# A product over 12500 entities in fp32: pieces of 4 tiles with a ramp and a taper against rounds of 2, 2, 2 and 1 tiles

## The reference

```python
entities = jnp.einsum('be,le->bl', entity_idxs, W)    # x 1024 x 12500, W 128 x 12500, fp32
s = jnp.sum(entity_idxs, axis=1)
s_safe = jnp.where(s != 0, s, 1.0)
scale = jnp.where(s != 0, 1.0 / s_safe, 1.0)
return entities * scale[:, None]
```

## Time and profile before

| | |
|---|---|
| median of 3 runs | 151.33 us |
| the profiled execution | 151.15 us, span 149.4 |
| TensorE matmul, weight load | 135.2 us (91%), 76.4 (51%), 785 each |
| VectorE, ScalarE, GpSimd | 94.5 us (63%), 84.1 (56%), 0.7 |
| DMA | 58.19 MB in 5719 packets, mean 390 GB/s |
| loads in `xw` | 20 of 2304 KB, median 16.3 us from issue to landing |

### The profile page before, as it was taken

How to read it: one execution, slowest core, us unless ns; L and a number is a source line. 1 busy time by engine, 2 the same in 40 slices (tenths; PEclk the granted TensorE clock), 3 DMA queues, 4 the chain that set the end, 5 groups by cost and what they waited for, 6 DMA issues and landing times.

```text
span 149.4 us, 2230 instructions
## 1 busy us (share of the span) xinstructions
PE 135.2 (91%) x785; PEld 76.4 (51%) x785; DVE 94.5 (63%) x110; ACT 84.1 (56%) x129; POOL 0.7 (0%) x13
## 2 busy tenths in 40 slices
PE   0597998799999999999999999999999999999960
PEld 0244654455555555555555655655555555665530
DVE  0471953746756845955954954864864778965593
ACT  3571852735735834844843854763763677955173
POOL 1000000000000000000000000000000000000000
PEclk9999999999999999999999999999999999999998
DMA  5999999999999999999999999999999999999022
GB/s 147 404 427 459 405 454 399 449 420 425 444 410 449 410 444 420 434 434 410 454 415 434 420 439 429 410 459 410 434 425 439 408 425 416 414 406 342 16 70 75
DMA packets 5719, 58.19 MB, mean 390 GB/s; under 512 B 638, under 2 KB 1534, under 8 KB 2514
## 3 DMA queue, kind: packets, MB, share of 16 engines
q1 hardware_dynamic: 5714, 58.13, 92.6%
HBM read 57.60 MB, written 0.52 MB: 389 GB/s over the span
## 4 chain that ended last, share of the span: by engine, by line
DMA 56%; PE 35%; DVE 4%; SPq 1%; issue 1%
DMA xw<-main 56%; PE acc L417 35%; DVE y_sum L366 2%; DVE low_max L320 1%; SPq L167 1%; DVE row_sum L363 0%; SPq L163 0%; SPq L165 0%; DVE row_sum L357 0%; DVE row_sum L360 0%; DVE any_low L396 0%; PE acc L470 0%; DVE inexact L398 0%
## 5 line engine op out<-in xcount | busy, mean ns | idle before, releaser
L417 PE MATMUL acc<-parts_main,xw 128*128 128x385 bf16 x640 | 108.2, 327 | 3.8 <-DMA xw<-main 3.0
L417 PEld LDWEIGHTS acc<-parts_main,xw 128*128 128x128 bf16 x640 | 61.3, 98 | 50.7 <-issue 8.4
L320 DVE TENSOR_REDUCE low_max<-xw 128x2048 uint16 x20 | 45.5, 2278 | 0.0
L243 ACT ACTIVATE parts_main<-xw 128x512 bf16<-128x512 bf16 x20 | 12.7, 635 | 47.0 <-DMA xw<-main 37.7
L309 DVE TENSOR_TENSOR w_rest<-xw 128x512 f32<-128x512 f32 x20 | 13.8, 692 | 40.0 <-DMA xw<-main 40.0
L250 ACT ACTIVATE act_out<-xw 128x2048 bf16<-128x2048 uint16 x20 | 37.9, 1893 | 0.0
L316 DVE TENSOR_TENSOR parts_main<-w_rest 128x512 bf16<-128x512 f32 x21 | 14.6, 695 | 0.7
L246 ACT ACTIVATE parts_main<-w_rest 128x512 bf16<-128x512 bf16 x21 | 13.3, 635 | 2.0
L417 PE MATMUL acc<-parts_short,xw_short 84*128 84x385 bf16 x8 | 2.7, 522 | 5.5 <-ACT parts_short L246 5.5
L320 DVE TENSOR_REDUCE low_max<-xw_taper 128x1 f32<-128x1024 uint16 (+1 forms) x6 | 6.1, 1038 | 1.4 <-DMA xw_taper<-ends 1.3
L250 ACT ACTIVATE act_out<-xw_taper 128x1024 bf16<-128x1024 uint16 (+1 forms) x6 | 5.4, 906 | 1.7 <-DMA xw_taper<-ends 1.6
(11 more groups left out here) (50 smaller groups left out, 38.2 us busy)
## 6 DMA issues: line engine op xcount, KB each, us to landing
xw<-main SPq DMA_DIRECT2D x20, 2304.0 KB, 16.3
xw_taper<-ends SPq DMA_DIRECT2D x2, 1024.0 KB, 24.9
x_final<-ends SPq DMA_DIRECT2D x3, 512.0 KB, 27.8
xw_taper<-ends SPq DMA_DIRECT2D x1, 1408.0 KB, 21.8
xw_ramp<-ends SPq DMA_DIRECT2D x1, 1280.0 KB, 7.5
xw_taper<-ends SPq DMA_DIRECT2D x1, 1280.0 KB, 18.8
xw_taper<-ends SPq DMA_DIRECT2D x2, 512.0 KB, 27.1
xw_ramp<-ends SPq DMA_DIRECT2D x1, 704.0 KB, 4.9
```

The costliest lines, as they stand in the source:

```text
L243: nc.scalar.activation(parts[0:rows, 0:n, 0:L], top(words, n), ACT.Copy)
L320: nc.vector.tensor_reduce(low_max[0:rows, bass.ds(col, 1)], low(words, n), AX.XY, ALU.max).then_inc(dve_checked, 1)
L417: return nc.tensor.matmul(acc[:, b, 0:N], x, parts, start=first, stop=last)
```

## The change

The pieces become a uniform loop. After the short tile and the first two W tiles (`w_first`), 13 rounds of four pieces with 2, 2, 2 and 1 x tiles follow (52 pieces, 91 tiles), each with the W tiles of the next piece (2, 2, 1 and 2). There are still four slots, now with buffers of the pieces' own sizes. Then come the last four W tiles alone (`w_alone`) and the last 6 x tiles, cut by banks as before. Ramp and taper are gone. TensorE's program text has 8 products for the short tile, 56 for a round, 48 for the final tiles, and ahead of them a loop of 12 products of a zeroed tile (`idle`) into `acc`, which the first real products overwrite. In the final part VectorE checks a quarter of the words and ScalarE three quarters, `finish` adds the parts of both banks of a pair in one instruction, and the last bank is scaled by VectorE.

```diff
+IDLE_PRODUCTS = 12
+ROUNDS = 13
+SLOT_X = (2, 2, 2, 1)
+SLOTS = len(SLOT_X)
+SLOT_W = SLOT_X[1:] + SLOT_X[:1]
+PIECES = ROUNDS * SLOTS
+LAST = 6
+FINAL = ((0, 2, 0, 6), (2, 4, 0, 6), (4, 6, 0, 6), (6, 7, 0, 6), (7, 8, 0, 4), (7, 8, 4, 6))
+PAIRS = ((0, 2), (2, 4), (4, 6), (6, 7), (7, 8))
+ALONE = LAST - SLOT_X[0]
...
+            nc.gpsimd.memset(idle[:, :], 0.0).then_inc(idle_set, 1)
...
+            sp.dma_start(xw_short[0:short, :], edge(0)).then_inc(short_in, 16)
+            sp.dma_start(w_first[:, :], edge(1)).then_inc(first_in, 16)
             for s in range(SLOTS):
-                load_main(s, s)
-            with sp.Fori(1, MAIN // SLOTS) as i:
+                sp.dma_start(xw[s][:, :], piece(0, s)).then_inc(loop_in[s], 16)
+            with sp.Fori(1, ROUNDS) as i:
                 for s in range(SLOTS):
                     m = SLOTS * i + s
+                    sp.wait_ge(products_done, used(m - SLOTS))
+                    sp.wait_ge(dve_checked, used(m - SLOTS))
+                    sp.wait_ge(act_checked, used(m - SLOTS))
+                    sp.dma_start(xw[s][:, :], piece(i, s)).then_inc(loop_in[s], 16)
+            sp.dma_start(w_alone[:, :], edge(2)).then_inc(alone_in, 16)
...
 # ScalarE
+            with act.Fori(0, ROUNDS) as i:
                 for s in range(SLOTS):
                     m = SLOTS * i + s
+                    act.wait_ge(loop_in[s], 16 * (i + 1))
+                    act.wait_ge(products_done, used(m + 1 - SLOTS))
+                    split(xw[s][:, XS[s]:], parts[(s + 1) % SLOTS], SLOT_W[s], (s + 1) % 2, unit_split(m + 1))
+                    act.wait_ge(act_checked, used(m - 2))
+                    low_sum(xw[s][:, XS[s] // 2:XS[s]], m + 1, (s + 1) % 2).then_inc(act_checked, 1)
+            act.wait_ge(alone_in, 16)
+            split(w_alone, parts_alone, ALONE, 1, ALONE_SPLIT)
...
+            check(0)
+            check(1)
+            scale(0)
+            check(2)
+            scale(1)
+            check(3)
+            check(4)
+            scale(2)
+            check(5)
+            scale(3)
 # VectorE
+            dve.wait_ge(alone_in, 16)
+            dve.wait_ge(top_parts_done, unit_split(PIECES - 1))
+            rest(w_alone[:, :], ALONE, 1)
+            lo(parts_alone, ALONE, 1, ALONE_SPLIT)
...
             def finish(pair):
                 b0, b1 = PAIRS[pair]
+                dve.wait_ge(bank_full, pair + 1)
+                row_sum_is_zero(b0, b1, ONES).then_inc(sum_step, 1)
+                add_parts(b0, b1).then_inc(y_summed, 1)
...
+            check(0)
+            check(1)
+            finish(0)
+            check(2)
+            finish(1)
+            check(3)
+            check(4)
+            finish(2)
+            check(5)
+            finish(3)
+            finish(4)
+            dve.wait_ge(inverse_done, len(PAIRS))
+            dve.wait_ge(y_summed, len(PAIRS))
+            nc.vector.tensor_scalar(y[:, BANKS - 1, :], y_sum[:, BANKS - 1, :], row_sum[:, BANKS - 1, 2:3], None,
+                                    ALU.mult).then_inc(y_last_ready, 1)
 # TensorE
+            pe.wait_ge(idle_set, 1)
+            with pe.Fori(0, IDLE_PRODUCTS):
+                nc.tensor.matmul(acc[:, 0, 0:N], idle[:, 0:P], idle[:, :], start=True, stop=True)
             pe.wait_ge(ones_set, 1)
             pe.wait_ge(short_in, 16)
+            wait_split(1)
+            multiply(xw_short[0:short, 0:B], 1, parts_short, rows=short, first=True).then_inc(products_done, 3)
+            with pe.Fori(0, ROUNDS) as i:
                 for s in range(SLOTS):
+                    wait_split(unit_split(SLOTS * i + s))
+                    pe.wait_ge(loop_in[s], 16 * (i + 1))
+                    multiply(xw[s][:, 0:XS[s]], SLOT_X[s], parts[s]).then_inc(products_done, 1)
+            wait_split(ALONE_SPLIT)
...
+            for k in range(NF):
+                pe.wait_ge(final_in[k], 16)
+                mm = last_tiles(k, last_parts, product)
+                if FINAL[k][3] == LAST:
+                    mm.then_inc(bank_full, 1)
```

More of the change, by code:

```diff
@@ L42, in pieces, with rec_kernel @@
         at += rows * cols
-    return table, at
-def rec_kernel(nc, main, ends, out, E):
+    return table
+def rec_kernel(nc, loop, ends, out, E):
     B, L = out.shape
@@ L49, in rec_kernel, with edge, piece @@
     short = E - (TILES + LAST) * P
-    table, _ = pieces(short, B, L)
+    table = edges(short, B, L)
     ONES = PARTS * L
     N = ONES + 1
[L53 to L59, removed]
+    NF = len(FINAL)
+    CHECKS = 1 + PIECES + NF
+    XS = [x * B for x in SLOT_X]
+    ROWS = [x * B + w * L for x, w in zip(SLOT_X, SLOT_W)]
+    AT = [sum(ROWS[:s]) for s in range(SLOTS)]
+    assert 0 < short <= P and N < 512 and SLOTS == 4
+    def edge(k):
         at, rows, cols = table[k]
         return ends[at:at + rows * cols].rearrange("(p f) -> p f", p=rows)
+    def piece(i, s):
+        return loop[i, P * AT[s]:P * (AT[s] + ROWS[s])].rearrange("(p f) -> p f", p=P)
     with ExitStack() as ctx:
@@ new lines, in _, with rest_of_round @@
+                load_full(edge(0)[:, 0:B], edge(0)[:, B:B + L], short)
+                for j in range(SLOT_X[0]):
+                    sp.wait_ge(full_used, j + 1)
+                    load_full(x_of(0, 0, j), edge(1)[:, j * L:(j + 1) * L])
+                def rest_of_round(i):
+                    for s in range(1, SLOTS):
+                        for j in range(SLOT_X[s]):
+                            sp.wait_ge(full_used, sum(SLOT_X) * i + sum(SLOT_X[:s]) + j + 1)
+                            load_full(x_of(i, s, j), w_after(i, s - 1, j))
@@ L235, in _ @@
+                with sp.Fori(1, ROUNDS) as i:
+                    rest_of_round(i - 1)
+                    for j in range(SLOT_X[0]):
+                        sp.wait_ge(full_used, sum(SLOT_X) * i + j + 1)
+                        load_full(x_of(i, 0, j), w_after(i - 1, SLOTS - 1, j))
+                rest_of_round(ROUNDS - 1)
+                wait_out()
                 sp.wait_ge(full_ready, BANKS)
@@ L290, in check_final @@
-            def check_final(k):
-                size = x_final[k].shape[1]
-                c = EDGE + MAIN + NT + k
-                act.wait_ge(final_in[k], 16)
-                act.wait_ge(act_checked, c - 1)
-                low_sum(x_final[k][:, size // 2:size], 1, c, c % 2)
-            pair = 0
-            for k, (b0, b1, j0, j1) in enumerate(FINAL):
-                check_final(k)
-                if k and FINAL[k - 1][3] == LAST:
-                    for b in range(*FINAL[k - 1][0:2]):
-                        scale(b, pair)
-                    pair += 1
@@ new lines, in check, with scale @@
+            def check(k):
+                act.wait_ge(final_in[k], 16)
+                act.wait_ge(act_checked, used(PIECES + k - 2))
+                low_sum(x_final[k][:, dve_share(k):], 1 + PIECES + k, (k + 1) % 2).then_inc(act_checked, 1)
+            def scale(pair):
+                act.wait_ge(inverse_done, pair + 1)
+                act.wait_ge(y_summed, pair + 1)
+                for b in range(*PAIRS[pair]):
+                    nc.scalar.activation(y[:, b, :], y_sum[:, b, :], ACT.Copy,
+                                         scale=row_sum[:, b, 2:3]).then_inc(y_ready, 1)
```

342 lines of the change are left out of this document (106 added, 236 removed).

## The result

The changed kernel takes 157.18 us, the median of 4 runs (153.27 to 163.21), against 151.34 (151.24 to 151.38) before; 148.6 had been forecast. It is slower, and its runs lie ten microseconds apart where those of before lie within 0.15. The ratio is 1.0145 (95% interval 1.0116 to 1.0173); it is taken over the fast runs of each kernel alone, here two of four, which is why the ratio of the medians, 1.039, is larger.

What follows compares the result with a forecast made beforehand. The DMA queue was taken as the limit up to 120.5 us, TensorE after. Savings of 1.35 at TensorE's end and 1.4 in the endings took 151.15 to 148.4, 148.6 as a median; range 147.2 to 150.8.

Steps and rivals of the forecast that it cites:

- Smaller ring: Loop slots: released 2.9 us after landing, full again at 7.3, due after 9.75; spare 2.4 us, cost 0.
- rival D: Loop: the ring runs dry, 12 us per microsecond over the spare 2.4; DMA activity below nine tenths; 154.6 at 0.5 over; 6%.
- Rival C: Loop: TensorE restarts at each of 52 pieces, rounds of 10.4 us, 8.5 us more, 157; chance 8%.
- the cover is gone if TensorE is over 2.4 us late: Loop slots: the spare 2.4 us cover a late engine, but no longer if TensorE is later than that.
- More, smaller pieces: Input transfers: 61 in place of 35; by a line of 0.0368 ns a byte plus 8 ns a row, last landing +1.65 us.
- rival B: Input transfers: the extra rows cost nothing because the queue hides it, rounds of 9.6 us, 147.0; chance 12%.
- Short TensorE program: TensorE's text: 113 products in place of 272, no instruction fetch delaying a loop landing, -1.25 us.
- Loop balance: Loop round of 7 tiles: DMA sets the pace at 9.75 us; TensorE needs 9.2, VectorE 7.5.
- The start: Start of the loop: the first loop piece was to land at 7.8 us.
- Zero products: Before the first weights: 12 zero products let first pieces run at 0.164 us a product; worth 0 by itself.
- The end of TensorE: Final products: start 3.3 us after T, the last loop piece's landing (131.65), and end at 143.0, -1.35 us.
- the endings: After TensorE's end E: last store starts at E + 1.45 in place of 2.85, -1.4 us.

Runs made afterwards that it cites:

- e5: The changed kernel run again without an edit: 157.53 us.
- e6: The changed kernel with the first two W tiles loaded after the first loop piece instead of before it: 154.43 us.
- e7: The changed kernel with a round's pieces side by side as column ranges of 32256-byte partition rows: 160.13 us.
- e12: The changed kernel with six more zero products between the short tile and the loop: 158.02 us.
- e1: The changed kernel without the 12 zero products: 159.12 us.
- e11: The changed kernel with seven of each tile's eight products in the loop, ring still 7 tiles, output partial: 151.27 us.
- e3: The changed kernel with two of each tile's eight products in the loop, ring still 7 tiles, output partial: 152.57 us.
- e2: The changed kernel with eight slots, a ring of 14 tiles, in place of four: 151.34 us.
- e9: The changed kernel with a ring of 14 tiles and the first W tiles loaded after the first loop piece: 150.51 us.
- e4: The kernel before with the 12 zero products added ahead of its first real ones: 151.12 us.
- e8: The kernel before with the changed kernel's new ending alone, 4 final tiles as before: 150.82 us.
- e10: The kernel before with the new ending and 6 final tiles in place of its two 1-tile taper pieces: 149.92 us.

## Why the prediction was wrong

The step that failed is "Smaller ring ... Cost 0". It had the release right (2.9 us; 3.0 measured) and asked the wrong question. It asked how soon a slot could be full again "with nothing queued": 1.0 to the first packet, 2.75, 0.6, so a spare of 2.4 us. But the queue is hardly ever empty here, and what counts is how long before its end a load must be in it. From the issue to the landing of the piece ahead there are 7.0 - 3.0 = 4.0 us; less the 0.6 for receipt, 3.4 us before the queue's last byte. By the 1.0 us of the first issue that leaves 2.4 to spare; the runs show none. The table has every profiled run with the new loop, rounds 2 to 13. "Held" is the time from a first piece's landing to its slot's reload, "lead" the landing of the piece ahead less the issue (median of first pieces), "late" a landing more than 0.1 us later than the piece's own transfer asks for, and "longest row" that of 9216 bytes (0.36 us when nothing is wrong):

| kernel, profiled run | held | lead | late first pieces | late of all 48 | longest row | median of all runs |
|---|---|---|---|---|---|---|
| after, 153.8 us | 3.0 us | 4.0 us | 5 of 12 | 8 | 1.8 us | 157.2 |
| e5, 154.0 | 3.0 | 4.0 | 1 | 10 | 1.3 | 157.5 |
| e6, 154.1 | 3.0 | 4.0 | 8 | 11 | 2.5 | 154.4 |
| e7, 154.4 | 3.0 | 4.2 | 5 | 10 | 2.0 | 160.1 |
| e12, 158.3 | 3.0 | 4.1 | 6 | 15 | 2.4 | 158.0 |
| e1, 159.7 | 3.0 | 4.0 | 10 | 14 | 2.4 | 159.1 |
| e11, 148.8 | 2.7 | 4.3 | 0 | 0 | 0.4 | 151.3 |
| e3, 153.4 | 2.3 | 4.7 | 0 | 0 | 1.6 | 152.6 |
| e2, 151.6 | | 13.7 | 1 | 2 | 0.8 | 151.3 |
| e9, 150.5 | | 13.1 | 1 | 1 | 0.8 | 150.5 |

The same dependence shows within the first six kernels, which do all the products. Of the first, second and third pieces of rounds 3 to 13, 37 of 68 are late when the lead was under 4.0 us, 11 of 51 at 4.0 to 4.2, 7 of 43 at 4.2 to 4.5, and 1 of 36 above. So it is no sharp threshold but a chance that falls with the lead.

Why a load needs that lead isn't shown, nor why the rows of a load that was issued late take longer. The start of a load alone doesn't explain it: in the packets of the changed kernel the first rows begin 1.0 us after the issues at 0.75 and at 14.85, when the queue had nothing else or almost nothing. The Trainium skill (DMA: Bandwidth & Descriptors, "Latency and other measured facts") gives some 600 ns to the first byte; the trace has 1.0 us, and with either there would be room to spare.

The prediction named this case as rival D, with 12 us for each microsecond over the spare, and gave it 6 in 100. Its form was right in part (a median of 157 is 0.7 over by that price), its chance not: the spare had been worked out from one row of the empty queue. Its sign, DMA activity below nine tenths, shows only between 11 and 19 us; in the rest of the loop the engines are busy with rows that take longer. Rival C had named 157 us, the very median, for another reason; that is a coincidence, as the undisturbed rounds of 9.78 us show.

In the profiled run the condition that the prediction itself had put, "the cover is gone if TensorE is over 2.4 us late", was met once: the first reload went out 5.35 us after its piece had landed, 2.45 later than forecast, and the 2.3 us lost in round 2 follow it. e12 takes that delay away and the late landings of the later rounds stay, so it isn't the whole.

The other steps:
- *More, smaller pieces*: right. Rounds of 9.78 against 9.75 from the line through three row sizes; rival B would have been 9.6. (The four pieces were put down as 2.75, 2.75, 2.6 and 1.55, which add up to 9.65; the line itself gives 2.78, 2.78, 2.63 and 1.57, and the runs 2.78, 2.78, 2.65 and 1.57.)
- *Short TensorE program*: right. No instruction packet lies in the loop (the one of q8 falls in the final part, at 144 us). The kernel before has one at 24 to 26 us in each of its profiled variants, e4, e8 and e10, beside a piece that is 1.2 to 1.6 us late; in e2 and e9, with a longer text, one is back at 25 us beside a round that is only 0.3 to 0.4 us longer. The Trainium skill (Runtime: NRT & Kernel Launch, "Instruction fetch mechanics") calls the crossing mostly hidden; beside these rounds it isn't.
- *Loop balance*, rival C: TensorE's first product of a piece starts within 0.1 us of the landing (9.54 after 9.50), and with ring 14 its pace allows rounds of 9.8. C falls.
- *The start*: mis-sized by 1.7 us. 7.8 for the first loop piece was what e11 shows; the runs of the same order of loads have 7.8, 9.2, 9.4, 9.5, 9.6, 9.75, 9.75 and 10.1. The slow rows are there too: the first piece's longest row is 0.6 us in e11 and 1.1 to 1.9 in the others. What makes them slow isn't shown.
- *Zero products*: 0 by themselves, right (e1, e4). But "the first pieces run at 0.164" failed in both profiled runs of the changed kernel. In the first the pace hadn't risen by then (the short tile's 8 products take 2.73 us as before); in e5 it had (1.47 us) and fell back in a wait of 2.07. The first reload went out at 14.85 and 15.12, later than the 12.5 that the prediction gave for a kernel without zeros.
- *The end of TensorE* and *the endings*: right, T + 3.0 for 3.3, E + 1.39 for 1.45. The new ending isn't worth its 1.4 us by itself (e8: 0.4 us; with 6 final tiles, e10: 1.2).

So of the 8.6 us between forecast and median, the profiled run shows 1.7 of a late start, 0.4 of longer rounds and 3.4 of late landings, less some 0.3 won behind the loop. The other 3.4 part that run from the median; by the traces of e1 and e12, long runs consist of more late landings.

## What to carry to other kernels

Size a ring by the lead of a load, and not only by whether the slot is free in time: add up what is queued behind the slot's piece when it is released, and keep well over 4 us of it where the transfers set the pace (4.0 was too little here, 4.3 barely enough, some 13 left nothing to see). Where a DMA-bound loop is at this edge, a small thing decides: one product in eight was worth 6 us. Runs that scatter by several us after a change to a ring are a sign to follow. GB/s below the neighbours in the page's slices shows the place; the DMA share need not, as a slow row counts as busy.

## What the runs showed of the hardware

TensorE's clock at the start differs from run to run of one kernel. In e5 the short tile's 8 products take 1.47 us; TensorE then idles 2.07 us before the first loop piece at 9.61, and the granted clock falls to the lower level (0.50, that is 1.2 GHz) and is back at 1.00 in the row of 16 to 18 us (not shown). In the same kernel's other profiled run those 8 products take 2.73 us and the first piece's are 0.33 us apart; the column says 1.00 there only because the trace has no record of the clock before 14.3 us. In e12 a wait of 1.58 us before 10.11 left the clock at 1.00. For TensorE's pace, count products in a window beside reading PEclk. Windows of e5:

```profile
10.00:12.00 2.00, 2.00 (x8) 0.96 (x7) 1.67 (x3) 1.55 (x4) 0.00 (x0) 0.50 1.00 416
12.00:14.00 2.00, 2.00 (x8) 0.90 (x6) 1.47 (x3) 1.46 (x3) 0.00 (x0) 0.50 0.95 395
14.00:16.00 2.00, 2.00 (x10) 1.00 (x9) 1.41 (x4) 1.33 (x5) 0.00 (x0) 0.68 0.17 69
```

There the DMA share of 14 to 16 us is 0.17 (69 GB/s): the first reload went out at 15.12. With the ring of 7, TensorE's slow clock at the first piece thus shows up as idle DMA engines five microseconds later.

A DMA row can take several times its normal time while the engines' share stays full (0.36 us normally; up to 2.5 in e6), so a full DMA share doesn't say that the DMA is at its best rate.
